# The group-norm's scale and shift computed on VectorE between its threshold passes, with only the power on GpSimd, and three transposed fills ahead of the control products

## What is computed

```python
x = jax.nn.relu(x)                                   # x here: _gn(x)
avg_region = jnp.mean(x, axis=(2, 3), keepdims=True)
peak_region = jnp.max(x, axis=(2, 3), keepdims=True)
x = jnp.where(peak_region - avg_region < 0.5, 0.0, x)
cmax = jnp.max(x, axis=1, keepdims=True)
cmean = jnp.mean(x, axis=1, keepdims=True)
bb = 1.0 - jnp.exp(-jnp.abs(cmax - cmean))
x = bb * x
x_max = jnp.max(x, axis=(2, 3), keepdims=True)
pooled = jnp.mean(x, axis=(2, 3))
control1 = jax.nn.sigmoid(pooled @ W1.T)[:, :, None, None]
control3 = jax.nn.relu(pooled @ W3.T)
control3 = jnp.where(control3 < 1.0, 1.2, control3)[:, :, None, None]
thres = control1 * control3 * x_max
return jnp.where(x < thres, 0.0, x)                  # layer: x + this
```

## Time and profile before

| what | before |
|---|---|
| device time, median of 3 runs | 1784.53 us (1778.58 to 1799.36) |
| the profiled execution's own time | 1780.24 us, its span 1778.4 us |
| VectorE busy | 1460.9 us, 82% |
| ScalarE busy | 1306.6 us, 73% |
| TensorE matmul busy | 1303.4 us, 73% |
| GpSimd busy | 610.6 us, 34% |
| HBM read, written | 310.38 MB, 205.52 MB (290 GB/s) |
| mean granted TensorE clock | 0.843 |

### The profile page before, as it was taken

One profiled execution on the slowest core, in us unless ns is written; L12 is line 12 of the kernel. 1 busy time (PEld: TensorE's weight loads), 2 busy tenths in 40 slices (PEclk: granted clock), 3 DMA queues, 4 the chain that ended last, 5 costly groups with the idle time before them and its releaser, 6 DMA issues.

```text
span 1778.4 us, 45243 instructions
## 1 busy us (share of the span) xinstructions
PE 1303.4 (73%) x19616; PEld 1080.2 (61%) x19616; DVE 1460.9 (82%) x2192; ACT 1306.6 (73%) x1921; POOL 610.6 (34%) x446
## 2 busy tenths in 40 slices
PE   4888776788876778767688777678777688777761
PEld 3766655666665666655576655566655566656660
DVE  2588887988887988888888887888887887888987
ACT  5678777777787878777767787777787767777821
POOL 0043233443233444223443233443233442233430
PEclk8898888998888898888888888898878887888885
DMA  9259989999999899998989999989999988899973
GB/s 396 87 162 301 319 315 320 281 296 297 312 330 336 277 285 306 302 329 320 287 263 296 307 330 332 283 277 296 301 330 329 279 265 269 315 329 343 296 228 145
DMA packets 93418, 518.86 MB, mean 292 GB/s; under 512 B 10272, under 2 KB 10272, under 8 KB 93216
## 3 DMA queue, kind: packets, MB, share of 16 engines
q1 hardware_dynamic: 75360, 416.38, 58.4%
q0 software_dynamic: 17856, 99.56, 28.7%
HBM read 310.38 MB, written 205.52 MB: 290 GB/s over the span
## 4 chain that ended last, share of the span: by engine, by line
PE 29%; POOL 26%; ACT 22%; DVE 15%; issue 7%; DMA 1%; SPq 0%; DVEq 0%; ACTq 0%; POOLq 0%
POOL xs L778 23%; ACT rs L476 8%; PE ps_turn L286 7%; PE ps_gate L347 7%; ACT xs L476 7%; PE ps_gate L322 6%; PE ps_gate L294 6%; DVE xs L670 6%; ACT rs L451 5%; DVE rs L670 4%; DVE max_and_mean L622 2%; POOL rstd L757 2%; DMA xs<-in_x 1%; PE ps_gate L356 1%; DVE xs L737 1%
## 5 line engine op out<-in xcount | busy, mean ns | idle before, releaser
L622 DVE TENSOR_REDUCE max_and_mean<-ps_turn 128x2 f32<-128x1024 f32 x384 | 466.0, 1220 | 201.3 <-PE ps_turn L286 200.6
L286 PE MATMUL ps_turn<-ident,xs 128*128 128x128 f32 (+1 forms) x1600 | 358.8, 310 | 177.7 <-DVE max_and_mean L622 112.3
L769 POOL DMA_DIRECT2D xs<-in_x x124 | 111.6, 968 | 940.0 <-DVE xs L670 837.0
L778 POOL TENSOR_TENSOR xs<-xs,rs 128x1568 f32<-128x1568 f32 x124 | 433.3, 3531 | 1.9 <-DVE rs L670 1.9
L286 PEld LDWEIGHTS ps_turn<-ident,xs 128*128 128x128 f32 (+1 forms) x1600 | 204.5, 153 | 311.5 <-DVE max_and_mean L622 155.2
L312 PE MATMUL ps_gate<-ident,bb 128*128 128x128 f32 (+1 forms) x1600 | 273.4, 333 | 153.2 <-ACT bb L469 144.0
L425 ACT ACTIVATE scratch<-xs 128x3136 bf16<-128x3136 f32 x128 | 360.2, 2814 | 7.8 <-DMA xs<-in_x 2.8
L312 PEld LDWEIGHTS ps_gate<-ident,bb 128*128 128x128 f32 (+1 forms) x1600 | 249.6, 239 | 173.4 <-DVE ymax_parts L639 157.7
L286 PE MATMUL ps_turn<-ident,rs 128*128 128x128 f32 (+1 forms) x1600 | 341.3, 299 | 6.0 <-issue 6.0
L639 DVE CUSTOM_DVE_ANT_0 xs<-xs,ps_gate 128x768 f32<-128x768 f32 (+1 forms) x256 | 243.3, 959 | 45.1 <-PE ps_gate L312 45.0
L451 ACT ACTIVATE xs<-xs,shift,rstd 128x3136 f32<-128x3136 f32 x64 | 191.9, 2999 | 100.0 <-POOL shift L761 93.3
(11 more groups left out here) (80 smaller groups left out, 991.9 us busy)
## 6 DMA issues: line engine op xcount, KB each, us to landing
xs<-in_x SPq DMA_DIRECT2D x260, 784.0 KB, 13.7
out<-xs SPq DMA_DIRECT2D x256, 784.0 KB, 8.2
xs<-in_x POOLq DMA_DIRECT2D x124, 784.0 KB, 11.1
rs<-in_L_conv_W SPq DMA_DIRECT2D x2, 1024.0 KB, 18.7
```

Of the source, the lines that this page charges most:

```text
L286: mm = pe.transpose(ps_turn[0:w, n % 2, b - 2 * i, P * t:P * (t + 1)], r_tile(s, t)[:, P * b:P * b + w], ident[:, :])
L622: ins = dve.tensor_reduce(max_and_mean[:, 2 * i:2 * i + 2, 0], ps_turn[:, n % 2, :, :], AX.X, ALU.max)
L778: pool.tensor_tensor(o, o, half(r_tile(s - 1, t), h), ALU.add).then_inc(added, 1)
```

## The change

Four edits.

1. **Scale and shift.** `affine` on GpSimd (six instructions) and `copy_group` on ScalarE are gone. VectorE does `variance(s)` (copy of the group sums from PSUM, minus the squared mean, add, maximum with zero plus epsilon) and later `shifts(s)`; GpSimd does only the power between them (`root(s)`).
2. **Order on VectorE and GpSimd.** On VectorE, `block_max 3`, `variance`, `block_max 4`, `shifts` now stand between `differ(s, 0)` and the fourth keep. On GpSimd `root(s + 1)` stands ahead of the wait for the four keeps.
3. **Control products.** The three first fills stand ahead of all products, which come in one piece.
4. **ScalarE.** The first tile's squares come in two halves, the first of them ahead of `control_exp`; their second sum is in a fifth column of `squares`, which TensorE adds by one more small matmul. One more `pool_sum` stands ahead of the last `relu`.

```diff
 def group_stats(s):
-    pe.wait_ge(squared, T * (s + 1))
-    pe.matmul(ps_group[:, 1, :], group_avg[:, :], squares[:, :], start=True, stop=True
-              ).then_inc(group_sums, 1)
+    pe.wait_ge(squared, (T + 1) * (s + 1))
+    first = LOAD_ORDER[0]
+    pe.matmul(ps_group[:, 1, :], group_avg[:, :], squares[:, 0:T], start=True, stop=False,
+              skip_group_check=True)
+    pe.matmul(ps_group[:, 1, first:first + 1], group_avg[:, :], squares[:, T:T + 1],
+              start=False, stop=True, skip_group_check=True).then_inc(group_sums, 1)
@@ TensorE's loop
     turn(s, 0)
-    if s > 0:
-        control_products(s - 1, range(0, 2))
     turn(s, 1)
-    if s > 0:
-        control_products(s - 1, range(2, T))
     turn(s, 2)
     if s > 0:
+        control_products(s - 1)
         control_logits(s - 1)
@@ ScalarE's loop
         copy_control(s - 1)
+    if has_next:
+        square_half(s + 1, 0)
+    if s > 0:
         control_exp(s - 1)
     if has_next:
-        square_tile(s + 1, 0)
+        square_half(s + 1, 1)
         square_tile(s + 1, 1)
...
     if has_next:
-        copy_group(s + 1)
         relu(s + 1, RELU_ORDER[0])
...
-    pool_sum(s, 0, 0)
+    for t in range(2):
+        pool_sum(s, 0, t)
     if has_next:
         relu(s + 1, RELU_ORDER[3])
@@ VectorE: new, and its loop
+def variance(s):
+    dve.wait_ge(group_sums, s + 1)
+    steps.step(dve.tensor_copy(gst[:, :, :], ps_group))
+    steps.wait()
+    steps.step(dve.scalar_tensor_tensor(gsq[:, :], gst[:, 0, :], -1.0, gst[:, 0, :],
+                                        ALU.mult, ALU.mult))
+    steps.wait()
+    steps.step(dve.tensor_tensor(gvar[:, :], gsq[:, :], gst[:, 1, :], ALU.add))
+    steps.wait()
+    dve.tensor_scalar(geps[:, :], gvar[:, :], 0.0, GN_EPS, ALU.max, ALU.add).then_inc(geps_ready, 1)
+
+def shifts(s):
+    dve.wait_ge(rstd_ready, s + 1)
+    dve.scalar_tensor_tensor(shift[:, :], gst[:, 0, :], -1.0, rstd[:, :], ALU.mult, ALU.mult
+                             ).then_inc(affine_ready, 1)
...
     differ(s, 0)
+    block_max(s, 3)
+    if s + 1 < B:
+        variance(s + 1)
+    block_max(s, 4)
+    if s + 1 < B:
+        shifts(s + 1)
     if s > 0:
         keep_tile(s - 1, KEEP_ORDER[3])
-    for i in range(3, 6):
-        block_max(s, i)
+    block_max(s, 5)
@@ GpSimd's loop, behind the four transfers of L769
-        pool.wait_ge(kept, T * s)
     if s + 1 < B:
-        affine(s + 1)
+        root(s + 1)
     if s > 0:
+        pool.wait_ge(kept, T * s)
         for t in KEPT_X:
```

More of the change, by code:

```diff
@@ L340, in count_fails, with control_products @@
                 mm.then_inc(count_ready, 1)
-            def control_products(s, products):
-                for k in products:
+            def control_products(s):
+                for k in range(T):
                     pe.wait_ge(pooled_ready, NS * T * s + T * (NS - 1) + k + 1)
@@ L487, in _ @@
             act.wait_ge(consts_ready, 1)
-            for n in range(T):
+            for h in range(2):
+                square_half(0, h)
+            for n in range(1, T):
                 square_tile(0, n)
             row_means(0)
-            copy_group(0)
             act.wait_ge(wt_ready, 2 * T)
@@ L523, in _ @@
                 gate_values(s, 3)
-                for t in range(1, T):
+                for t in range(2, T):
                     pool_sum(s, 0, t)
@@ L670, in keep_tile @@
                 dve.scalar_tensor_tensor(r, r, thres[:, t:t + 1], r, ALU.is_ge, ALU.mult).then_inc(kept, 1)
+            variance(0)
+            shifts(0)
             peaks(0)
@@ L747, in _, with root @@
             pool.wait_ge(consts_ready, 1)
-            def affine(s):
-                pool.wait_ge(group_copied, s + 1)
-                steps.step(pool.tensor_tensor(gsq[:, :], gst[:, 0, :], gst[:, 0, :], ALU.mult))
-                steps.wait()
-                steps.step(pool.tensor_tensor(gvar[:, :], gst[:, 1, :], gsq[:, :], ALU.subtract))
-                steps.wait()
-                steps.step(pool.tensor_scalar(geps[:, :], gvar[:, :], 0.0, GN_EPS, ALU.max, ALU.add))
-                steps.wait()
-                steps.step(pool.tensor_tensor(rstd[:, :], geps[:, :], half_neg[:, :], ALU.pow))
-                steps.wait()
-                steps.step(pool.tensor_tensor(mrs[:, :], gst[:, 0, :], rstd[:, :], ALU.mult))
-                steps.wait()
-                pool.tensor_scalar(shift[:, :], mrs[:, :], -1.0, 1.0, ALU.mult, ALU.mult).then_inc(affine_ready, 1)
-            affine(0)
+            def root(s):
+                pool.wait_ge(geps_ready, s + 1)
+                pool.tensor_tensor(rstd[:, :], geps[:, :], half_neg[:, :], ALU.pow).then_inc(rstd_ready, 1)
+            root(0)
             for s in range(B):
```

34 lines of the change are left out of this document (15 added, 19 removed).

## The result

| what | before | after |
|---|---|---|
| device time, median | 1791.42 us (1778.58 to 1799.36, 4 runs) | 1906.49 us (1901.87 to 1910.7, 4 runs) |
| the profiled execution's own time, its span | 1780.24, 1778.4 us | 1907.06, 1905.3 us |
| VectorE, ScalarE, TensorE, GpSimd busy | 82, 73, 73, 34% | 78, 69, 70, 30% |
| mean granted TensorE clock | 0.843 | 0.826 |
| HBM rate | 290 GB/s | 271 GB/s |

The change makes the kernel slower: ratio 1.065, 95% interval 1.057 to 1.073. The prediction was 1822, with 1862 as its upper end; the time lies 44 us beyond that.

The account below looks back on a forecast made before the run. The prediction took a loop through all four engines as the bound. 13 x 0.7 + 17 x 1.7 + 2 = +40 on 1780.24 gave 1820, stated as 1822 us; eight-in-ten range 1792 to 1862.

Parts of the forecast that it names:

- The loop that bounds the kernel: A chain through TensorE, GpSimd, ScalarE and VectorE, once a period from threshold to threshold; 51.33 us plain, 54.62 stopped.
- the adds at +18.8: GpSimd's adds start 18.8 us behind the threshold in plain periods, before 16.5; 2.36 us later.
- the keep: VectorE's fourth keep, now behind variance and shift, starts at +15.3 instead of +10.5 behind the threshold.
- the clock's rise 4 us into the fills: TensorE's fills run unbroken from 994.03, so its clock rises at 998.0, within the third fill.
- the tail of 19.2: From GpSimd's adds to the next threshold: 19.2 us instead of 20.9 or so, returning 1.66 of the 2.36.
- the length of a plain period: Period without a TensorE stop in sum_x: +0.7 us each, 13 counted.
- the sign: The whole kernel gets slower, above 1802 us; chance 0.72.
- The term at the start: Once, VectorE does weights first, then variance and shift, and the first relu waits: about +2 us.
- the stopped periods: Periods where TensorE stops in sum_x with no semaphore to wait for: 17, a stop costing 3.0 us, +1.7 each.
- the rival of the vanishing stops: Longer TensorE program puts its stops elsewhere; none at all gives 1752 us, faster by 1.6%; chance 0.09.
- The tail did take back what it could: Rival at adds to threshold: an earlier clock rise recovers the delay; 1800 us with two or three stops fewer; chance 0.19.
- The fourth case: Worse than forecast: late fourth transfer issue on GpSimd or clock low through TensorE's products; 1860 to 1880 us; chance 0.17.

Follow-up runs that it names:

- e1: Kernel before with only the three first fills moved ahead of all control products; 1812.44 us, ratio 1.017.
- e13: Kernel before with only the ScalarE edit: first tile's squares in halves, one more small matmul, one more sum ahead of the last relu; 1818.77 us, ratio 1.016.
- e6: Kernel after with the control products put back behind the first and second fills; 1891.02 us, ratio 1.060.
- e7: Kernel before with the second group-statistics matmul done twice, four more TensorE records per image; 1791.97 us, ratio 1.003.
- e4: Kernel after with GpSimd's accumulating transfers carrying 128 of their 1568 columns; 1784.58 us, one run.
- e9: Kernel before with GpSimd's accumulating transfers carrying 128 of their 1568 columns; 1733.64 us, one run.
- e10: Kernel after with the fourth keep ahead of maximum 3 and variance again, and the shift reading the mean from PSUM; 1796.11 us, ratio 1.007.

## Why the prediction was wrong

**What held.** The loop that bounds the kernel, the adds at +18.8, the keep, the power, the clock's rise 4 us into the fills (in the one period shown), the tail of 19.2 (19.25), the length of a plain period (51.36 + 0.7 = 52.1, measured 52.19, but over three periods only) and the sign. How the tail gets there did not hold: the prediction added up unbroken fills and one sum less, and each of edits 3 and 4 gives the whole of it alone (19.0 in e1, 19.3 in e13, 19.0 in e6). In stopped periods the adds start 5.6 behind the group sums (before 2.8), where 6.2 less the 0.47 by which the sums come later, 5.7, was forecast. The term at the start was +2 and is +0.9: the threshold's line in after, its first and last start:

```profile
L683 DVE TENSOR_TENSOR thres<-control x32: 161/163/165, 103.2 to 1872.6; 128x4 f32<-128x4 f32 x32
```

**What failed** is above all one term: the stopped periods. The prediction took over their number (17) and the stop's cost (3.0). The 129 us of the 30 periods are, with the prediction's own terms:

- 14 x 0.7 + 16 x 1.7 = 37: the sum as it stood.
- 11 more stopped periods. By the forecast a stopped one is 54.66 + 1.7 = 56.36, a plain one 52.06: 11 x 4.3 = 47.
- 27 x (58.01 - 56.36) = 45: the stopped ones are longer than forecast. The group sums end at +19.06 on average, against +16.78 before. Forecast were 0.47 later, measured 2.3. Of the 1.8 between them 0.7 are longer pauses (3.34 against 2.62). The rest is about what the low clock costs: ahead of the end of the sums TensorE spends 3.8 us of a stopped period at 1.2 GHz in after (in 25 of the 27), 1.4 before (in 7 of the 16), and at half speed the 2.4 between them are 1.2 us of work.

Together 129.

The same in the terms of the adds: before, they start at +16.5 or 2.8 behind the end of the group sums, whichever is later; after, always 5.6 behind it. Over the 30 periods the sums end at +14.99 on average before and at +18.53 after, where 14.99 + 0.47 = 15.46 was forecast. The 3.07 between them, 30 times, are the 92 us that the sum lacks.

**The step that failed** is that the stops were carried over as they were. Its reason stands in the rival of the vanishing stops: "each position in a period is met at some time, and a shift of length changes only when". True as far as length goes (e7). But from it I took that the number would stay, and allowed three more or fewer: 27 periods stopped instead of 16, and at 58.01 us instead of 56.36. Which positions stop was not a property of the program. It depended on when a block is asked for and when the loads end, against the start of the accumulating transfers at +5.7, and the change moved the first by 0.5 us (in the two periods compared) and the second by 0.7. I had seen pauses with nothing to wait for, and priced them, without asking what TensorE was waiting for.

A smaller step failed beside it. The 0.7 of a plain period was worked out on one where the sums came early, 12.8 behind the threshold, and taken for all. Before, later sums up to +13.7 cost nothing; after, each delay goes through. By e4 and e9 the change costs 51 us without the big pauses, where 30 x 0.7 + 2 = 23 was forecast for that case.

**The rivals.** The tail did take back what it could, and the shorter tail brought the stops, which no case had. By itself this is cheap: with the keep at its old place and no lock (e10) 27 periods stop too, and the 30 periods take 21 us more than before (1614.3 against 1593.7). It is the keep behind them, 108.5 us, that makes the stops dear. The fourth case gave 1860 to 1880 and named low clock and late transfers; neither was the cause as it meant them (a clock low through the products, a late fourth issue), though a low clock behind the pause carries part of the last term. The stops did move, to the other side.

**What stays open.** Why a block waits behind the accumulating transfers is not shown; that it does, and that fewer bytes or a later start of them take most stops away, is. That the tail moves the pauses by way of the loads is argued from the landings and the counts, and no run moved the loads alone. e4 and e9 move less data in all, so the loads can be helped by them too.

## What to carry to other kernels

An engine that stops with nothing to wait for waits for something that the view doesn't name. Count its instructions: pauses at multiples of 256 are its own program arriving late, and what helped here was in the transfers that run then, not in the engine. Before a cheap pause is carried over into a sum, ask what decides it, since here a shift of the schedule by half a microsecond switched it on nearly everywhere. And ask what slack a new order takes away: a delay that cost nothing before can cost its whole length after. And on VectorE a small instruction with two SBUF inputs must not stand beside GpSimd's long ones: with one operand in PSUM it took 162 ns instead of 3458.

## What the runs showed of the hardware

- A 16.4 KB block of TensorE's program started 0.9 us behind the crossing with few other transfers, and 3.6 to 4.6 us with accumulating ones (4.1 in the median of before and of after; 1.1 and 1.3 with these transfers thinned); execution went on 2.2 to 3.6 us behind its start, 2.35 in the median of 340 pauses. `sum_x` needs one every 3.4 to 3.8 us.
- With 17856 accumulating packets of 99.56 MB TensorE stood 81.5 us in `sum_x`, with the same number at 8.13 MB 9.1 us.
- A VectorE instruction on 128x4 took 3.46 us instead of 0.16 beside a GpSimd add, with both inputs in SBUF.
- After a pause of 2.8 us the granted clock was 0.59 for the 4.0 us that followed, at 1.2 GHz from 0.7 us behind the pause on.
